# Rows of a graph network's tables as three exact bf16 pieces in layers two and three

## What is computed

```python
def _sage_layer(x, src, dst, inv_deg, W_self, W_neigh, b):
    agg = jax.ops.segment_sum(x[src], dst, num_segments=N_NODES)
    mean = agg * inv_deg[:, None]
    return x @ W_self + mean @ W_neigh + b
deg = segment_sum(ones_like(src), dst)
inv_deg = 1.0 / jnp.maximum(deg, 1.0)
```

## Time and profile before

| | us |
|---|---|
| time, median of 3 runs (lowest, highest) | 4305.91 (4305.18, 4308.22) |
| the profiled execution | 4308.08 |
| its span, first to last instruction | 4306.3 |
| layer two, first gather to the first of layer three | 1018.77 to 2000.08 |
| layer three, first to last gather of its table | 2000.08 to 2982.1 |
| attention gathers | 2995.0 to 4018.2 |
| the rest: feed forward and output | to 4306.3 |

### The profile page before, as it was taken

One profiled execution on the slowest core, in us unless ns is written; L12 is line 12 of the kernel. 1 busy time (PEld: TensorE's weight loads), 2 busy tenths in 40 slices (PEclk: granted clock), 3 DMA queues, 4 the chain that ended last, 5 costly groups with the idle time before them and its releaser, 6 DMA issues. The chain is left out here.

```text
span 4306.3 us, 75198 instructions
## 1 busy us (share of the span) xinstructions
PE 3277.9 (76%) x13728; PEld 2372.7 (55%) x13729; DVE 2147.4 (50%) x6078; ACT 487.8 (11%) x1111; POOL 3020.7 (70%) x3154
## 2 busy tenths in 40 slices
PE   3777777777777777777788778887777777776798
PEld 2565555555555555555566555565655555555544
DVE  6434333333333333333455555545577777777733
ACT  4000000000000000000011101101011111111122
POOL 5777777777777777777777777776777777777200
PEclk9888889898888888888999999999888889898999
DMA  6444434435344344344444444445655555554411
GB/s 202 121 136 124 124 106 124 125 105 143 105 125 125 105 125 124 106 125 127 130 140 136 142 136 136 142 135 155 162 147 157 148 159 147 157 146 138 127 60 60
DMA packets 284796, 563.69 MB, mean 131 GB/s; under 512 B 104638, under 2 KB 176133, under 8 KB 279691
## 3 DMA queue, kind: packets, MB, share of 16 engines
q0 software_dynamic: 150528, 414.45, 34.0%
q10 hardware_dynamic: 70180, 89.46, 6.3%
q1 hardware_dynamic: 63974, 58.59, 4.4%
HBM read 487.19 MB, written 73.45 MB: 130 GB/s over the span
## 5 line engine op out<-in xcount | busy, mean ns | idle before, releaser
L763 POOL DMA_INDIRECT arena<-h_table,idx_v x2292 | 2174.3, 949 | 726.3 <-issue 694.0
L895 PE MATMUL banks<-arena 128*128 x5856 | 1544.9, 420 | 617.9 <-SPq L790 506.0
L895 PEld LDWEIGHTS banks<-arena 128*128 128x128 f32 x5856 | 1171.5, 208 | 957.2 <-issue 774.4
L842 DVE TENSOR_SCALAR arena<-iota_t,dst_e 128x128 f32<-128x128 f32 x2928 | 846.8, 310 | 821.7 <-PE banks L895 575.9
L1278 POOL DMA_INDIRECT arena<-vs_table,idx_v x764 | 765.0, 1001 | 232.8 <-issue 228.8
L1496 PE MATMUL banks<-arena 128*128 x1952 | 518.8, 416 | 52.8 <-DVE arena L1840 52.6
L1496 PEld LDWEIGHTS banks<-arena 128*128 128x128 f32 x1952 | 366.5, 199 | 192.5 <-issue 120.4
L916 PE MATMUL banks<-arena,lhs 128*128 128x256 f32 x1176 | 339.6, 439 | 5.0 <-ACT lhs L1016 0.2
L948 DVE TENSOR_SCALAR small<-banks 128x1 f32<-128x1 f32 x147 | 23.2, 158 | 638.7 <-PE banks L897 638.7
L1016 ACT ACTIVATE lhs<-banks 128x512 f32<-128x512 f32 x147 | 87.8, 597 | 2073.7 <-PE banks L907 2073.5
L916 PEld LDWEIGHTS banks<-arena,lhs 128*128 128x128 f32 x1176 | 240.5, 215 | 100.8 <-ACT lhs L1016 64.8
(11 more groups left out here) (263 smaller groups left out, 2468.4 us busy)
## 6 DMA issues: line engine op xcount, KB each, us to landing
arena<-h_table,idx_v POOLq DMA_INDIRECT x2292
arena<-dst_dram SPq DMA_DIRECT2D x14, 1792.0 KB
arena<-vs_table,idx_v POOLq DMA_INDIRECT x764
h_table<-arena ACTq DMA_DIRECT2D x11, 1024.0 KB, 7.4
h_early<-arena ACTq DMA_DIRECT2D x10, 1024.0 KB
vs_table<-arena ACTq DMA_DIRECT2D x49, 132.0 KB
x_dram<-arena ACTq DMA_DIRECT2D x49, 128.0 KB
hln_dram<-arena ACTq DMA_DIRECT2D x49, 128.0 KB
```

Of the source, the lines that this page charges most:

```text
L763: pool.indirect_dma_start(ring[:, s * BJ + j, 0:width], None, table, bass.IndirectOffsetOnAxis(idx_v[:, half, n * BJ + j:n * BJ + j + 1], ...
L842: dve.tensor_scalar(onehot[:, j, :], iota_t[:], dst_e[:, bass.ds(b * BJ + j, 1)], None, ALU.is_equal).then_inc(W["onehot_made"], 1)
L895: pe.matmul(agg[:, 0:D + 1], onehot[:, j, :], ring[:, (b % SLOTS) * BJ + j, 0:D + 1], start=False, stop=False).then_inc(W["onehot_used"], 1)
```

## The change

In layers two and three a row is stored and gathered as three bf16 pieces whose sum is the fp32 row: 3 x 256 x 2 B = 1536 B instead of 1024 B. PE multiplies a bf16 matrix of ones and zeros with pieces one and two in one matmul of 512 columns (two halves of the PSUM bank), and with piece three in one of 256 columns onto the second half; `means` adds the halves. The degree's reciprocal is kept from layer one. Layers one and two write the pieces: ACT writes the first with a second activation, DVE the other two (`split_vector`, three instructions for each tile). There are two buffers of pieces, so each tile is stored by itself, early and full table, and the store of tile t-1 (`store_parts`) stands in ACT's step of tile t, behind `take_turned(t)`. The late rows are added piece by piece: 12 rounds instead of 4. The core of the diff:

```diff
-    tables = [dram(f"h_table{i}", (NP, D)) for i in range(3)]
-    early_tables = [None] + [dram(f"h_early{i}", (NP, D)) for i in range(1, 3)]
+    PARTS = 3
+    PW = PARTS * D // 2
+    tables = [dram("h_table0", (NP, D))] + [dram(f"h_table{i}", (NP, PW)) for i in range(1, 3)]
+    early_tables = [None] + [dram(f"h_early{i}", (NP, PW)) for i in range(1, 3)]
...
-        LAST_STORES = 16 * (NT // GS + 2)
+        LAST_STORES = 16 * NT
...
-            pe.wait_ge(W["h_made"], since("h_made", l, 0))
-            for b in range(LATE):
-                if b > 1:
-                    pe.wait_ge(late_added, 2 * ((l - 1) * LATE + b - 1))
+            pe.wait_ge(parts_made, parts_at(l - 1, NT))
+            for r in range(LATE * PARTS):
+                b, m = r // PARTS, r % PARTS
+                if r > 1:
+                    pe.wait_ge(late_added, 2 * ((l - 1) * LATE * PARTS + r - 1))
                 for j in range(BJ):
-                    last = pe.matmul(banks[:, late_banks(l, b)[j // 2], (j % 2) * D:(j % 2 + 1) * D],
-                                     late_rows[:, b, j * P:(j + 1) * P], h_nodes[:, NT - 1, :], start=True, stop=True)
+                    last = pe.matmul(banks[:, late_banks(l, r)[j // 2], (j % 2) * D:(j % 2 + 1) * D],
+                                     late_rows[:, b, j * P:(j + 1) * P], parts[:, (NT - 1) % 2, m, :], start=True, stop=True)
...
+        def split_vector(dve, l, t):
+
+            hi, mid, lo = (parts[:, bass.ds(t % 2, 1), m, :].rearrange("p o d -> p (o d)") for m in range(PARTS))
+            dve.wait_ge(W["h_made"], since("h_made", l, t + 1))
+            dve.tensor_tensor(left_over, h_nodes[:, t, :], hi, ALU.subtract).then_inc(part_step, 1)
+            dve.wait_ge(part_step, PARTS_FROM + 2 * (l * NT + t) + 1)
+            dve.tensor_copy(mid, left_over).then_inc(part_step, 1)
+            dve.wait_ge(part_step, PARTS_FROM + 2 * (l * NT + t) + 2)
+            dve.tensor_tensor(lo, left_over, mid, ALU.subtract).then_inc(parts_made, 1)
...
-                     turned=NT, lhs_made=NT, out_done=NT, h_made=NT, stored=16 * (NT // GS + 1), landed=16 * BJ * ROUNDS)
+                     turned=NT, lhs_made=NT, out_done=NT, h_made=NT, stored=16 * (NT - 1), landed=16 * BJ * ROUNDS)
...
-                    dve.tensor_scalar(onehot[:, j, :], iota_t[:], dst_e[:, bass.ds(b * BJ + j, 1)], None,
+                    to, ids = (onehot, iota_t[:]) if w == 0 else (hot16, iota16)
+                    dve.tensor_scalar(to[:, j, :], ids, dst_e[:, bass.ds(b * BJ + j, 1)], None,
                                       ALU.is_equal).then_inc(W["onehot_made"], 1)
...
-            gathers(pool, l, D, may_fill)
+            gathers(pool, l, D if l == 0 else PW, may_fill)
...
+                            pe.matmul(agg[:, 0:2 * D], hot16[:, j, :],
+                                      ring_parts[:, (b % SLOTS) * BJ + j, 0:2, :].rearrange("p m d -> p (m d)"), start=False, stop=False)
+                            last = pe.matmul(agg[:, D:2 * D], hot16[:, j, :], ring_parts[:, (b % SLOTS) * BJ + j, 2, :],
+                                             start=False, stop=False)
+                        last.then_inc(W["onehot_used"], 1)
...
+                dve.tensor_scalar(small_parts, agg[:, D:2 * D], inv_deg[:, bass.ds(t, 1)], None, ALU.mult).then_inc(W["deg"], 1)
+                dve.wait_ge(W["deg"], 2 * NT + (l - 1) * NT + t + 1)
                 wait(dve, W["turned"], since("turned", l, t))
-                dve.tensor_scalar(mean[:], agg[:, 0:D], small[:, 1:2], None, ALU.mult).then_inc(W["mean_made"], 1)
+                dve.scalar_tensor_tensor(mean[:], agg[:, 0:D], inv_deg[:, bass.ds(t, 1)], small_parts, ALU.mult, ALU.add).then_inc(W["mean_made"], 1)
...
             def step(t):
                 onehots(dve, l, t, *base_and_span(dve, l, t))
+                if there(t - 1):
+                    split_vector(dve, l, t - 1)
                 means(t)
...
+            def store_parts(t):
+                act.wait_ge(parts_made, parts_at(l, t + 1))
                 if not isinstance(t, int) or t < NT - 1:
-                    act.dma_start(early[:, bass.ds(t, n), :], h_nodes[:, bass.ds(t, n), :]).then_inc(W["stored"], 16)
-                act.dma_start(to[:, bass.ds(t, n), :], h_nodes[:, bass.ds(t, n), :]).then_inc(last_stored[l], 16)
+                    act.dma_start(early[:, bass.ds(t, 1), :], parts_f[:, bass.ds(t % 2, 1), :]).then_inc(W["stored"], 16)
+                act.dma_start(to[:, bass.ds(t, 1), :], parts_f[:, bass.ds(t % 2, 1), :]).then_inc(last_stored[l], 16)

             def step(t):
                 own_rows(t)
                 take_turned(t)
+                if there(t - 2):
+                    act.wait_ge(W["stored"], since("stored", l, 16 * (t - 1)))
+                    act.wait_ge(last_stored[l], 16 * (t - 1))
+                if there(t - 1):
+                    store_parts(t - 1)
...
                 act.wait_ge(W["out_done"], since("out_done", l, t + 1))
                 apart(act)
+                act.activation(parts[:, bass.ds(t % 2, 1), 0, :].rearrange("p o d -> p (o d)"), dense[:, 0:D], ACT.Relu)
                 act.activation(h_nodes[:, t, :], dense[:, 0:D], ACT.Relu).then_inc(W["h_made"], 1)
```

More of the change, by code:

```diff
@@ L721, in late_rows_vector @@
         def late_rows_vector(dve, l):
-            for b in range(LATE):
-                dve.wait_ge(landed[b], since("landed", l, 16 * BJ))
-                dve.wait_ge(late_found, l * LATE + b + 1)
+            for r in range(LATE * PARTS):
+                b, m = r // PARTS, r % PARTS
+                if m == 0:
+                    dve.wait_ge(landed[b], since("landed", l, 16 * BJ))
+                dve.wait_ge(late_found, LATE + (l - 1) * LATE * PARTS + r + 1)
                 for i in range(2):
-                    rows = ring[:, b * BJ + 2 * i:b * BJ + 2 * i + 2, 0:D]
-                    dve.tensor_tensor(rows, rows, banks[:, late_banks(l, b)[i], :].rearrange("p (j d) -> p j d", d=D),
+                    rows = ring_parts[:, b * BJ + 2 * i:b * BJ + 2 * i + 2, m, :]
+                    dve.tensor_tensor(rows, rows, banks[:, late_banks(l, r)[i], :].rearrange("p (j d) -> p j d", d=D),
@@ L829, in base_and_span @@
                 dve.wait_ge(W["onehot_made"], since("onehot_made", w, (b0 + t) * BJ))
-            dve.tensor_scalar(iota_t[:], iota_n[:], tile_base[:, bass.ds(t, 1)], None, ALU.add).then_inc(W["base_moved"], 1)
+            dve.tensor_scalar(iota_t[:] if w == 0 else iota16, iota_n[:], tile_base[:, bass.ds(t, 1)], None, ALU.add).then_inc(W["base_moved"], 1)
             return b0, b1
@@ L889, in sums @@
                 wait(pe, W["mean_made"], since("mean_made", l, t))
-                pe.matmul(agg[:, 0:D + 1], zeros[:, 0:P], zeros[:, 0:D + 1], start=True, stop=False)
+                width = D + 1 if l == 0 else 2 * D
+                pe.matmul(agg[:, 0:width], zeros[:, 0:P], zeros[:, 0:width], start=True, stop=False)
                 with pe.Fori(b0, b1 + 1) as b:
@@ L970, in step @@
                 onehots(dve, l, t, *base_and_span(dve, l, t))
+                if there(t - 1):
+                    split_vector(dve, l, t - 1)
                 means(t)
             def last_layer_step(t):
+                if isinstance(t, int) and t == 3:
+                    dve.wait_ge(last_stored[1], LAST_STORES)
                 def between():
@@ L1064, in sage_scalar @@
             if l < 2:
-                first_and_rest(act, GS, step)
-                store(0, GS)
+                step(0)
+                step(1)
+                with act.Fori(2, GS) as t:
+                    step(t)
                 if l == 0:
                     late_setup_scalar(act)
-                with act.Fori(1, NT // GS - 1) as g:
-                    with act.Fori(g * GS, g * GS + GS) as t:
-                        step(t)
-                    store(g * GS, GS)
-                with act.Fori(NT - 1 - GS, NT - 2) as t:
-                    step(t)
-                store(NT - 1 - GS, GS - 1)
-                step(NT - 2)
-                store(NT - 2)
-                step(NT - 1)
-                store(NT - 1)
+                with act.Fori(GS, NT) as t:
+                    step(t)
+                store_parts(NT - 1)
             else:
```

66 lines of the change are left out of this document (46 added, 20 removed).

## The result

The changed kernel takes **4340.14 us** (median of 4 runs, 4336.36 to 4342.4) against 4305.73 for the kernel before in the same comparison: a ratio of 1.0078, 95% interval 1.006 to 1.0095. It is slower, as forecast. The predicted 4328.4 is 11.7 us too low, and the median lies 0.1 us above the range's upper end. The profiled execution took 4341.48 with a span of 4339.7, 33.4 us longer than before.

A forecast was written before the change was run, and what follows sets the result against it. POOL was taken to pace the kernel; 11.0 + 11.5 + 0.3 - 0.3 = 22.5 us on the median of 4305.91 gave 4328.4 us, with an 8-in-10 range of 4321 to 4340.

The forecast's parts named there:

- What bounds the kernel: Whole kernel: POOL's gathers, one every 1.252 us, pace the layers and PE waits for rows; delays of gathers add one for one.
- PE's term of zero: Inside layers two and three: the bf16 products' changed time on PE doesn't reach POOL, cost 0.
- the prediction's 0.50 and its third: PE's products: each of 1952 loses perhaps 0.17 us, a third of 0.50 us at full clock.
- PE was the bound: Rival, layers two and three: PE sets the pace, faster products save 332 us, 3996 us with the stalls; chance 0.02.
- Start of layer two: POOL waits for tile 47's store, now behind tile 48's copy: +11.0 us, bounds 10.4 to 11.7.
- Start of layer three: Same wait for the late store, with faster products and later wide rows counted: +11.5 us, bounds 10 to 14.
- The ring's cover: Start of layer two: late rows' 12 rounds barely free the first block before POOL needs it; +0.3 us, bounds 0 and 5.
- the ring's cover is gone: Rival, layer starts: late rows end later, POOL stops before the eighth block, 3 to 8 us each, 4332 to 4344; chance 0.09.
- Attention start: POOL's existing 12.91 us wait there shortens through faster products in the last tile's sum: -0.3 us, bounds -1 and +1.
- A gather of 1536 B takes longer: Rival, layers two and three: gather time grows in proportion to bytes, +742 us, 5070 us; chance 0.01.
- Inside the layers: Products, narrower comparisons, DVE's split (1.1 us a tile) and ACT's extra work stay hidden behind POOL: cost 0.
- DVE holds POOL up: Rival, layers one and two: the split's 108 us of DVE work stops POOL, +82 us, 4410 us with stalls; chance 0.04.

The follow-up runs named there:

- the mended kernel: Changed kernel with store ahead of the copy, earlier split and split from PSUM together, on slower chips: ratios 0.9852 and 0.9815 to the kernel before there.
- e1: Changed kernel with ACT's store of tile t-1 ahead of the copy of tile t's transposed rows: 4330.47 us, ratio 1.0052.
- e2: Changed kernel with the store ahead of the copy and DVE's split of tile t-1 behind tile t's first block's comparisons: 4319.53 us, ratio 1.0026.
- e5: Kernel before with only tile 47's store in layers one and two moved behind tile 48's copy: 4328.75 us, ratio 1.0042.
- e3: Changed kernel with the split's remainder in PSUM, so neither subtraction has two SBUF operands; late store left: 4329.81 us, ratio 1.0046.
- g1: Changed kernel with e1 to e3, plus one PSUM operand in queries times keys and the attention stage's 256-column comparison: 4306.04 us, ratio 0.9994.
- g2: Kernel before with one PSUM operand in layer three's queries times keys and the attention stage's 256-column comparison: 4304.66 us, ratio 0.9991.
- f1: Changed kernel with e1, e2 and e3 together, on a slower chip: 6425.56 us against 6551.62 for the kernel before there, ratio 0.9815.

## Why the prediction was right, and where it was short

- **What bounds the kernel** (POOL paces the layers): right. PE's term of zero held. Products that follow one another directly start every 0.32 to 0.38 us instead of every 0.43 at the granted clock of 1.0 (2.4 GHz), and every 0.64 instead of 0.86 at 0.5 (1.2 GHz); that is a quarter less at most, and the prediction's 0.50 and its third were too much. PE's busy time in layer two falls from 735.38 to 706.64 us, and the granted clock from 0.86 to 0.81; POOL sees none of it. The rival "PE was the bound" is out on this chip, but on the slower chips, where POOL waits 1500 us for blocks, the mended kernel does gain.
- **Start of layer two**, +11.0 forecast, **+10.7** measured. The copy of tile 48 came 7.5 us after POOL asked (7.2 by the earlier trace rows), the store was issued 0.5 us after the copy's start and not after its end, and the store's trip was 2.7 us and not 3.2. e1, e2 and e5 show the cause.
- **Start of layer three**, +11.5 forecast, **+9.6** measured, under the lower bound of 10. The working took 1.0 us off for the bf16 products and gave 0.3 back; the copy came 6.4 us after POOL asked instead of 8.3, so 1.9 us were saved, and the trip was again 2.7 us. The 0.3 for wider rows was right: PE starts 2.8 us after POOL asks instead of 2.5. The four products took 1.6 us instead of 3.8, which is 2.2 saved and not 1.0: the granted clock from them to the copy is 1.00 in the changed kernel and 0.50 before.
- **The ring's cover**, +0.3 forecast, **0** measured: first product 29.6 us behind the first gather, forecast 32. The rival "the ring's cover is gone" didn't come about in the changed kernel; it does, with 0.8 to 2.6 us at layer two, in e1, e2, e3 and g1, so the worry was sound. It is the only rival whose range, 4332 to 4344, holds the measured time, but by another cause: that the time came out within 0.1 us of the range, whose upper part was kept for this rival, is luck.
- **Attention start**, -0.3 forecast, 0 measured (12.90 against 12.91).
- **A gather of 1536 B takes longer**: refuted, the median stays 946 ns, and g1's gathers take no longer than g2's with their 1024 B (742.0 against 742.8 us in layer two, 741.6 against 742.4 in layer three). The times (4306.04, 4304.66) leave 1.4 us for everything in the change once mended. That is less than the waits which g1 has over g2, 1.1 and 1.5 us at the two starts, 2.3 before the eighth block of layer two and 2.7 early in the attention stage; the stages' own scatter hides the rest.
- **Inside the layers, cost 0 ("Hidden")**: this is the step that failed. It asked only whether DVE's split delays PE, which it doesn't. The prediction's rival "DVE holds POOL up" had the right mechanism and the wrong condition. It was set aside because layer three of the kernel before has instructions with two SBUF operands and still takes 982.02 us; but a gather is longer, by up to 0.25 us, only when it begins in about the first 0.2 us of that instruction, and before only 5 gathers of layer three did. Nor was it right that the trace shows nothing of it at 256 columns: those 5 take up to 1.18 us, and 48 of the attention stage's long gathers lie under a comparison of 256 columns. A total of 784 gathers hides that; the list of the long ones, by what ran over their start, doesn't.
- **What stands in its place**: not zero, but 8.7 us in the three layers and 4.4 behind them, 13.1 together. Of the layers' part e3 shows the split's share (its long gathers vanish in layers one and two; in the changed kernel they are 5.6 us too long together); the share of L1220 is shown in g1, where layer three's go from 29 to 0 (they are 5.5 us too long together, 0.8 before). It could have been priced from rows: 196 new subtractions with two SBUF operands, 0.42 us each, on a grid of 1.25 us, so a gather would begin under one in three of them if they stood at random on that grid; 65 such gathers at 0.25 us are an estimate of 16 us at most. 50 came, 25 of them long.
- **The attention stage**, also put at no change behind its start: that it is 4.4 us longer, with 144 long gathers instead of 152, is again a matter of where the instructions stand on POOL's grid, as far as the groups show (the gathers under one scan are 10.5 us too long together instead of 7.2, those under another 6.3 instead of 3.7). No run separates it, and the stage moves as much by itself: its instructions are the same in the kernel before, the changed one, e1, e2, e3 and e5, and it takes 1021.7 to 1027.8 us in their profiles, the changed kernel's being the longest. So 4.4 us may be this execution's and not the change's.

The sum of 22.5 was thus 2.2 us too high in the stalls and left out 13.1; 20.3 + 13.1 = 33.4.

The Trainium skill, "SBUF — State Buffer", section "Who interferes with whom", says that a VectorE instruction with two SBUF inputs contends with a GpSimd instruction that reads SBUF. The traces agree, and give the price: up to 0.25 us for a gather. They differ from its remark that such a `tensor_tensor` leaves descriptor generation alone, which the page itself calls inferred: the long gathers under L763 take 1.17 to 1.20 us, and with one operand in PSUM all take 0.94 to 0.95.

## What to carry to other kernels

When one engine issues transfers back to back and sets the pace, count its instructions that are longer than the median and look at what the other engines ran at their start, before calling added work hidden; and place work with two SBUF operands on VectorE, if it must be there, with one operand in PSUM. When a store is moved behind a wait in an engine's program, ask who waits for the store: here the waiting copy needed POOL's own last rows, and 20 us came of one line's place. Where the pace is set by another engine, as on the slower chips here, the same edits are worth something else; a verdict on work off the path holds for the chip that it was taken on.

## What was not expected of the hardware

- A gather's time on POOL doesn't depend on its width: 946 ns median for 1024, 1056 and 1536 B a row, one every 1.25 us, although the gathers' queue moves a quarter more bytes (517.21 MB against 414.45).
- The price of a collision depends on who starts first: of two DVE subtractions over neighbouring gathers, the one that began after the gather cost nothing, the one 0.04 us ahead cost 0.24 us. When the two start within 0.05 us, it can be the DVE instruction that is longer, 0.47 to 0.50 us instead of 0.42.
- Two of the four chips of the experiments ran the same program 1.52 times as long, with the single instruction as fast as ever. In f1's layer two a product's records still have 0.39 and 0.27 us and a gather 0.94, but between them DVE and PE wait for what the profile calls "remote" or "issue":

```profile
1606.27 0.94 POOL L798 DMA_INDIRECT arena<-h_table,idx_v  x1 [9.08 <-SPq L816]
...
1613.50 0.39 PE L936 MATMUL banks<-arena 128*128 x1 [0.55 <-issue]
1614.75 0.37 PE L938 MATMUL banks<-arena 128*128 x1 [0.87 <-issue]
1614.88 0.25 DVE L878 TENSOR_SCALAR arena<-iota_t,dst_e 128x128 bf16<-128x128 int16 x1 [1.20 <-remote]
```

```profile
DVE arena L878 <- remote: 620.4, 231, 5.1
```

In the changed kernel on the first chip no "remote" stands among DVE's seven largest waits. The mean granted clock is lower there too, 0.73 in f1 against 0.87 in the changed kernel and 0.90 in g1; no run shows whether that is a part of the cause or comes of the waits. What these waits are, and why two chips have them, stays open.
